# Full-array products and transposes as two column tiles of 64, and a new order of steps on all engines

## The chip, the cores and the metric

The kernel runs on one core of one Trainium2 chip. The metric is the time of one execution on the device, in microseconds (us), all input and output transfers between the chip's memory and the core included. Of several executions the median counts.

## The reference

Four layers follow one another on 16 images of 64 channels and 16 x 16 pixels, all in f32. The first is attention over channels, the second a deformable 3 x 3 convolution, the third attention over pixels, the fourth a block of normalisation, depthwise convolution, four gated one-dimensional convolutions and a gated feed-forward part.

```python
# L0: attention over channels
q, k, v = (einsum('oc,bcn->bon', w, x) + b for (w, b) in (q, k, v))
attn = softmax(einsum('bcn,bdn->bcd', q, k) / sqrt(64))
x = x + einsum('bcd,bdn->bcn', attn, v)
# L1: deformable 3x3 convolution, batch norm, relu
om = conv3x3(x, w_off) + b_off                  # 18 offsets and 9 masks per pixel
sampled = bilinear(x, grid + tap + om[:18]) * sigmoid(om[18:])
x = relu(batch_norm(einsum('bckhw,ock->bohw', sampled, w_dcn) + b_dcn))
# L2: attention over the 256 pixels
q, k, v = (einsum('oc,bcn->bon', w, x) + b for (w, b) in (q, k, v))
attn = softmax(einsum('bci,bcj->bij', q, k) / 8)
x = x + einsum('oc,bcn->bon', wp, einsum('bij,bcj->bci', attn, v)) + bp
# L3
y = depthwise3x3(ln2d(x)) + dw_b
o = sum over left-right, right-left, top-bottom, bottom-top of conv5(y) * sigmoid(G y + g)
x = x + fuse(o)
z = ff1(ln2d(x)); a, g = split(z)
x = x + ff2(a * sigmoid(g))
```

## The kernel before, in words

Two images make a pair: 2 x 64 channels fill the 128 partitions and 256 pixels lie in the free dimension, so 8 pairs (n = 1 to 8) go through the same steps. There is no loop over pairs. `PLAN` (lines 53 to 124) holds for each of the four engines one list of tokens such as `qk.4`, a step and its pair; `walk` (146) plays the list in that order, and the steps of several pairs are interwoven in it. Between engines every step waits on counting semaphores. SyncE (SP) loads the parameters, then for n = 3 to 8 loads pair n (333) and, from n = 6 on, first stores pair n - 5 (337).

TensorE's (PE's) steps and what they fill, with the lines of their products:

- `prep` (357, 358): once, the product of the weights v_w and p_w and of p_w with a bias. It needs the last parameter transfer, `par_late`.
- `qk` (366), `attn` (375), `at` (383), `mix` (390, 391), `x1` (397): layer 0. `at` transposes the normalised attention matrix, `mix` multiplies it with wv and leaves one 128 x 128 matrix that `x1` applies to both images.
- `off` (407), `off_t` (415): the offset convolution in nine taps and two halves, and its transpose. From it DVE (`dist`, `hat`, `hat_y`, and `low` once), ACT (`tanh`, `abs`, `high`) and POOL (`low`) make hat functions of the sampling positions, as an f16 high part and an f16 remainder in the tile `parts`.
- `tr0`, `tr1`, `tr2` (431): these parts transposed to `hats`, eight, eight and four f16 transposes of 128 x 128.
- `wx0`, `wx1`, `wx2` (446): x1 times the weights of the nine taps.
- `sp0` to `sp8` (`spread`, 460 and 455): selector products that spread the hats over all pixels, in f16 with 32 rows. ACT copies one of the two factors out (`xe`, 702), DVE multiplies them (`w0a` to `w8b`, 863), two products of 128 x 512 per tap.
- `s0a` to `s8b` (500): per tap and half two products, one for each image, that sum the samples in `cv`. `relu` (709) closes layer 1.
- `qk2` (511, 512), `v2` (521), `logit` (532), `et0` and `et1` (542, four f32 transposes each), `av` (553): layer 2.
- `gate` (564), `scan` (577), `fuse` (586), `ff` (597), `ff2` (605): layer 3. Its statistics and normalisation take DVE (`st1`, `st2`), POOL (`ln1`, `ln2`) and ACT (`ln1`, `ln2`), the depthwise taps ACT (`dw`) and DVE (`dw2` to `dw8`, `y`), and `x3`, `x4`, `prod`, `u` and `out` are DVE's.

A product uses part of the 128 x 128 array according to its operands: rows by the partitions it sums over, columns by the partitions it writes. In the profile "128*64" stands for 128 rows and 64 columns. This program uses four such shapes: 128*128 (prep, qk, x1, off_t, tr, qk2, v2, et), 128*64 (attn, at, off, s, av, fuse, ff2: two column tiles side by side, except at), 64*128 (mix, wx, logit, gate, scan, ff: two row tiles but for mix) and 32*128 (sp). An f32 product shows as two records, an f32 or f16 transpose as one. `nc.tensor.transpose` passes the data through in one pass, `nc.tensor.matmul` with an identity multiplies.

PSUM is small: nearly all steps of layers 0, 2 and 3 share the bank `mb` or the two banks `pair`. `turn` (151) lets a step write its bank only when the step before it in PE's list that used the same bank has been read by its last reader (`DONE`, 130):

```python
    turns = [entry for entry in entries(PLAN["pe"]) if entry[0] in BANK[bank]]
    at = turns.index((step, n))
    if at > 0:
        name, m = turns[at - 1]
        eng.wait_ge(semaphores[DONE[name]], m)
```

## Time and profile before

| | us |
|---|---|
| median of 3 runs | 326.28 |
| lowest, highest | 324.72, 327.69 |
| the profiled execution | 325.18 |
| its span, from the first to the last instruction | 323.3 |

All rows of the trace come from the one profiled execution and count from its span's start. The engines are PE (TensorE, matmul), PEld (its weight loads, which overlap PE), DVE (VectorE), ACT (ScalarE), POOL (GpSimd) and SP (SyncE). L500 is line 500 of the kernel. PE's records are drawn longer than the time for which one holds the engine back, because products are pipelined; the distance from the start of one step to the start of the next, or a piece of the chain of waits, is the better measure. The chain of waits is the work that ended last, followed back from the last instruction.

### The profile page before, as it was taken

How to read it: one execution, taken by the hardware profiler on the slowest of the kernel's cores; microseconds unless marked ns; L12 is line 12 of the kernel's file. 1: busy time of each engine (PE TensorE's matmuls, PEld its weight loads, DVE VectorE, ACT ScalarE, POOL GpSimd, SP SyncE). 2: the span in 40 equal slices, each digit the busy share in tenths (PEclk: the TensorE clock that was granted, in tenths of full speed). 3: DMA queues.
4: the chain of work that ended last, by engine and by line, in shares of the span. 5: the costliest groups of instructions: out<-in, count | busy, mean ns of one | idle time of the engine just before them, and what ended most of it. 6: DMA issues, size and time to landing. Idle time of an engine off the chain costs nothing.

```text
span 323.3 us, 6448 instructions
## 1 busy us (share of the span) xinstructions
PE 288.7 (89%) x2396; PEld 175.6 (54%) x2396; DVE 213.0 (66%) x422; ACT 192.4 (59%) x399; POOL 55.8 (17%) x139
## 2 busy tenths in 40 slices
...
GB/s 248 84 16 2 16 2 20 0 2 2 0 0 2 4 1 2 0 34 0 2 1 34 3 0 2 32 2 1 2 2 16 3 0 18 1 0 2 16 0 32
DMA packets 3053, 4.91 MB, mean 15 GB/s; under 512 B 336, under 2 KB 2768, under 8 KB 2896
## 3 DMA queue, kind: packets, MB, share of 16 engines
...
q14 instruction: 10, 0.08, 0.1%
...
## 4 chain that ended last, share of the span: by engine, by line
PE 74%; DVE 10%; ACT 6%; DMA 4%; issue 3%; POOL 1%; SPq 1%; DVEq 0%; POOLq 0%; ACTq 0%
PE ps_cv L500 20%; PE ps_pair L577 10%; PE ps_yb L460 7%; PE ps_pair L446 5%; PE ps_ma L407 4%; PE ps_mb L542 3%; PE ps_pair L532 3%; PE ps_ma L431 3%; PE ps_pair L564 3%; DMA sb_par<-in_par 2%; PE ps_pair L597 2%; PE ps_mb L553 2%; DVE sb_dw_acc L904 2%; DVE sb_wt L863 2%; PE ps_mb L586 2%
## 5 line engine op out<-in xcount | busy, mean ns | idle before, releaser
L863 DVE TENSOR_TENSOR sb_wt<-ps_yb,sb_xe 128x512 f32<-128x512 f32 x144 | 94.1, 686 | 34.1 <-PE ps_xb L455 32.8
L500 PE MATMUL ps_cv<-sb_wt,sb_w_x 128*64 128x256 f32 x576 | 81.2, 393 | 0.6 <-DVE sb_wt L863 0.5
L702 ACT ACTIVATE sb_xe<-ps_xb 128x512 f32<-128x512 f32 x72 | 42.9, 595 | 13.6 <-PE ps_xb L455 13.5
L500 PEld LDWEIGHTS ps_cv<-sb_wt,sb_w_x 128*64 128x64 f32 x576 | 34.4, 136 | 26.2 <-issue 12.6
L577 PE MATMUL ps_pair<-sb_y_pad,sb_par 64*128 64x256 f32 x320 | 37.6, 385 | 0.0
L999 POOL TENSOR_TENSOR sb_parts<-sb_hat,sb_parts 128x256 f16<-128x256 f32 (+2 forms) x40 | 24.3, 639 | 73.6 <-ACT sb_parts L672 73.6
L577 PEld LDWEIGHTS ps_pair<-sb_y_pad,sb_par 64*128 64x128 f32 x320 | 30.1, 186 | 7.1 <-issue 2.8
L904 DVE SCALAR_TENSOR_TENSOR sb_dw_acc<-sb_z_pad,sb_par,sb_dw_acc 128x256 f32<-128x256 f32 x56 | 26.1, 506 | 11.3 <-ACT sb_dw_acc L754 7.5
L460 PE MATMUL ps_yb<-sb_hats,sb_sel 32*128 32x512 f16 x144 | 29.8, 384 | 1.5 <-DVE sb_wt L863 1.1
L455 PE MATMUL ps_xb<-sb_hats,sb_sel 32*128 32x512 f16 x72 | 27.7, 385 | 0.1
L1006 POOL TENSOR_SCALAR sb_sc<-sb_mv 128x1 f32<-128x1 f32 x16 | 4.4, 277 | 133.5 <-DVE sb_mv L898 77.2
L446 PE MATMUL ps_pair<-sb_par,sb_x 64*128 64x256 f32 (+1 forms) x192 | 23.6, 362 | 0.7 <-ACT sb_w_x L692 0.6
L681 ACT ACTIVATE sb_hats<-ps_ma 128x1024 f16<-128x1024 f16 (+1 forms) x24 | 21.1, 880 | 4.7 <-PE ps_ma L431 4.6
L692 ACT ACTIVATE sb_w_x<-ps_pair 128x1024 f32<-128x1024 f32 (+1 forms) x24 | 19.4, 809 | 7.5 <-PE ps_pair L446 7.2
L460 PEld LDWEIGHTS ps_yb<-sb_hats,sb_sel 32*128 32x128 f16 x144 | 7.2, 91 | 23.4 <-issue 20.1
L446 PEld LDWEIGHTS ps_pair<-sb_par,sb_x 64*128 64x128 f32 x192 | 15.5, 186 | 7.2 <-issue 6.1
L407 PE MATMUL ps_ma<-sb_x_pad,sb_par 128*64 128x128 f32 x288 | 18.7, 287 | 0.6 <-DVE sb_x_pad L825 0.6
L407 PEld LDWEIGHTS ps_ma<-sb_x_pad,sb_par 128*64 128x64 f32 x288 | 16.8, 144 | 3.0 <-DVE sb_x_pad L825 1.8
L731 ACT ACTIVATE sb_b_exp<-ps_pair,sb_b_neg 128x256 f32<-128x256 f32 x32 | 14.7, 476 | 4.9 <-DVE sb_b_neg L872 4.9
L770 ACT ACTIVATE sb_conv<-ps_pair,sb_par 128x512 f32<-128x512 f32 x16 | 10.1, 682 | 9.2 <-PE ps_pair L577 9.2
L597 PE MATMUL ps_pair<-sb_z,sb_par 64*128 64x256 f32 x64 | 10.2, 439 | 5.9 <-ACT sb_z L777 4.0
L834 DVE TENSOR_TENSOR sb_dist<-ps_ma,sb_grid 128x1152 f32<-128x1152 f32 x8 | 10.8, 1352 | 5.7 <-PE ps_ma L415 5.6
...
## 6 DMA issues: line engine op xcount, KB each, us to landing
...
```

The costliest lines, as they stand in the source:

```text
L407: mm = nc.tensor.matmul(ma[C * h:C * (h + 1), 0:P], par_sb[:, a + 2 * OM * t:a + 2 * OM * (t + 1)], x1_pad[:, r:r + HALF_ROWS, t % 3:t % 3 ...
L446: mm = nc.tensor.matmul(pair[:, 512 * b + PIX * h:512 * b + PIX * h + k], x1[r, P * h:P * (h + 1)], par_sb[r, a:a + k], start=True, stop=True)
L455: return nc.tensor.matmul(xb[:, :], sel_sb[rows, P:2 * P], hats[n % 2][rows, g, :], start=True, stop=True)
L460: return nc.tensor.matmul(yb[h][:, :], sel_sb[rows, P * (2 + h):P * (3 + h)], hats[n % 2][rows, g, :], start=True, stop=True)
L500: mm = nc.tensor.matmul(cv[C * b:C * (b + 1), 0:PIX], w_x[n % 2][:, b, h, k, :], wt_of(n, k, h)[:, PIX * b:PIX * (b + 1)], start=(k == 0 a ...
L577: mm = nc.tensor.matmul(pair[:, 512 * b + PIX * d:512 * b + PIX * (d + 1)], par_sb[r, a:a + P], rows, start=(j == 0), stop=(j == KS - 1))
L681: nc.scalar.activation(hats[n % 2][:, g0:g1, :].rearrange("p g q -> p (g q)"), ma[:, :].bitcast(F16)[:, 0:k], ACT.Copy).then_inc(ev(f"hats ...
L692: nc.scalar.activation(w_x[n % 2][:, :, :, t0:t1, :].rearrange("p b h t c -> p b h (t c)"), pair[:, :].rearrange("p (b h q) -> p b h q", b ...
L702: nc.scalar.activation(xe[t % XE][:, :], xb[:, :], ACT.Copy).then_inc(ev("xe_ok"), 1)
L863: nc.vector.tensor_tensor(wt_of(n, k, h)[:, :], yb[h][:, :], xe[t % XE][:, :], ALU.mult)\
L904: nc.vector.scalar_tensor_tensor(out=sum_of, in0=dw_source(t), scalar=col("dw_w", t), in1=sum_of, op0=ALU.mult, op1=ALU.add).then_inc(ev(f ...
L999: nc.gpsimd.tensor_tensor(parts[:, 0:g, a:b, 1, :], hat[:, 0:g, a:b, :], parts[:, 0:g, a:b, 0, :], ALU.subtract).then_inc(ev("low_ok"), 1)
```

## The change

Seven kinds of PE steps that used the full array now issue each product twice, for columns 0 to 63 and 64 to 127 of the stationary operand, into partitions 0 to 63 and 64 to 127 of PSUM: prep, qk, x1, off_t, tr, qk2, v2. mix does the same and sums over 128 rows instead of 64; for that `at_sb` has 128 rows, whose lower half a sixth memset on DVE clears. at and off_t use a product with the identity instead of the transpose. et0 and et1 keep the full array. The f16 transposes of tr stay transposes, each as two of half width.

All four lists of `PLAN` hold the same tokens as before in a new order. Below are the lines of the lists that matter here, then the whole code part.

```diff
     "pe": """
-        qk.1 attn.1 prep.1 at.1 mix.1 x1.1 off.1 off_t.1 qk.2 attn.2 wx0.1 qk.3 wx1.1 at.2 tr0.1 wx2.1 mix.2 sp_first.1
 ...
-        scan.2 sp1.5 qk2.4 s0a.5 s0b.5 at.6 logit.4 mix.6 sp2.5 tr2.5 x1.6 s1a.5 off.6 sp3.5 fuse.2 off_t.6 s1b.5 wx1.6
-        v2.4 sp4.5 s2a.5 s2b.5 wx0.6 sp5.5 s3a.5 s3b.5 et0.4 s4a.5 wx2.6 sp6.5 et1.4 ff.2 s4b.5 s5a.5 s5b.5 sp7.5 gate.3
 ...
-        ff2.5 s7b.8 sp_last.8 av.7 s8a.8 s8b.8 scan.6 qk2.8 logit.8 fuse.6 v2.8 et0.8 gate.7 et1.8 ff.6 av.8 scan.7
-        ff2.6 gate.8 fuse.7 scan.8 ff.7 fuse.8 ff.8 ff2.7 ff2.8
+        qk.1 attn.1 at.1 mix.1 x1.1 prep.1 off.1 off_t.1 qk.2 attn.2 wx0.1 wx1.1 qk.3 tr0.1 at.2 mix.2 wx2.1 sp_first.1
 ...
+        attn.6 gate.2 qk2.4 tr2.5 s0b.5 sp2.5 s1a.5 at.6 mix.6 logit.4 fuse.2 s1b.5 sp3.5 x1.6 s2a.5 off.6 wx1.6 sp4.5
+        et0.4 off_t.6 wx2.6 v2.4 wx0.6 sp5.5 et1.4 s2b.5 ff.2 s3a.5 s3b.5 av.4 ff2.2 sp6.5 gate.3 s4a.5 s4b.5 s5a.5
 ...
+        s7a.8 av.7 s7b.8 sp_last.8 gate.6 s8a.8 ff2.5 s8b.8 scan.6 qk2.8 logit.8 fuse.6 v2.8 et0.8 gate.7 et1.8 av.8
+        ff.6 scan.7 ff2.6 gate.8 fuse.7 scan.8 fuse.8 ff.7 ff.8 ff2.7 ff2.8
     """,
     "act": """
-        attn.1 prep.1 at.1 mix.1 off.1 tanh.1 abs.1 attn.2 wx0.1 high.1 wx1.1 at.2 tr0.1 wx2.1 mix.2 xe0.1 tr1.1 xe1.1
 ...
-        exp0.8 v2.8 exp1.8 ln2.6 et0.8 gate.7 et1.8 ff.6 ln1.8 dw.8 scan.7 gate.8 ln2.7 scan.8 ff.7 ln2.8 ff.8
+        attn.1 at.1 mix.1 prep.1 off.1 abs.1 tanh.1 attn.2 wx0.1 high.1 wx1.1 at.2 tr0.1 mix.2 xe0.1 tr1.1 xe1.1 wx2.1
 ...
+        k2.8 exp0.8 v2.8 exp1.8 et0.8 et1.8 gate.7 ln2.6 ff.6 ln1.8 dw.8 scan.7 gate.8 ln2.7 scan.8 ff.7 ln2.8 ff.8
     """,
     "dve": """
-        qk.1 a_max.1 a_norm.1 x1.1 dist.1 qk.2 a_max.2 hat.1 hat_y.1 qk.3 a_norm.2 low.1 w0a.1 x1.2 w0b.1
 ...
-        w4b.5 w5a.5 y.3 hat.6 hat_y.6 w5b.5 w6a.5 u.2 w6b.5 out.2 w7a.5 x3.4 st1.4 qk.7 w7b.5 w8a.5 dw2.4 dw4.4 dw3.4
-        out.6 x4.7 st2.7 prod.8 x4.8 st2.8 u.7 out.7 u.8 out.8
+        qk.1 a_max.1 a_norm.1 x1.1 dist.1 qk.2 a_max.2 hat.1 hat_y.1 a_norm.2 low.1 qk.3 x1.2 a_max.3 w0a.1 w0b.1
 ...
+        w3b.5 w4a.5 dw2.3 dist.6 dw4.3 dw6.3 w4b.5 w5a.5 dw8.3 dw3.3 dw5.3 hat.6 dw7.3 u.2 x3.4 y.3 st1.4 out.2 hat_y.6
+        dw4.8 dw5.8 dw6.8 dw7.8 dw8.8 out.6 y.8 prod.7 x4.7 st2.7 prod.8 x4.8 st2.8 u.7 out.7 u.8 out.8
     """,
     "pool": """
-        grid.1 x1.1 bn.1 low.1 x1.2 low.2 x1.3 low.3 x1.4 ln1.1 low.4 ln1.2 x1.5 low.5 ln2.1
-        ln1.3 x1.6 ln2.2 low.6 ln1.4 ln2.3 x1.7 low.7 x1.8 ln1.5 ln2.4 low.8 ln1.6 ln2.5 ln1.7
-        ln2.6 ln1.8 ln2.7 ln2.8
+        x1.1 grid.1 bn.1 low.1 x1.2 low.2 x1.3 x1.4 low.3 low.4 ln1.1 ln1.2 x1.5 ln2.1 low.5 ln1.3 x1.6 ln2.2 ln1.4
+        low.6 ln2.3 x1.7 low.7 x1.8 ln1.5 ln2.4 low.8 ln1.6 ln2.5 ln1.7 ln2.6 ln1.8 ln2.7 ln2.8
     """,
 ...
@@ -188,7 +186,7 @@
         a_sum = sb("a_sum", [P, 1])
         a_rec = sb("a_rec", [P, 1])
         a_nrm = sb("a_nrm", [P, C])
-        at_sb = sb("at", [C, P])
+        at_sb = sb("at", [P, P])
         mix = sb("mix", [P, P])
         mix_b = sb("mix_b", [P, 1])
         x1 = sb("x1", [P, PIX])
@@ -350,21 +348,30 @@
             ident = part("ident")
             ident16 = sel_sb[:, 0:P]
 
+            def columns_of(t):
+                return slice(C * t, C * (t + 1))
+
             def prep(n):
                 if n == 1:
                     pe.wait_ge(par_late, 16)
                     turn(pe, S, "mb", "prep", n)
-                    nc.tensor.matmul(mb[:, 0:P], part("v_w"), part("p_w"), start=True, stop=True)
-                    nc.tensor.matmul(mb[:, P:P + 1], part("p_w"), col("v_b"), start=True, stop=True)\
-                        .then_inc(prep_mm, 1)
+                    for t in range(2):
+                        nc.tensor.matmul(mb[columns_of(t), 0:P], part("v_w")[:, columns_of(t)], part("p_w"),
+                                         start=True, stop=True)
+                    for t in range(2):
+                        mm = nc.tensor.matmul(mb[columns_of(t), P:P + 1], part("p_w")[:, columns_of(t)], col("v_b"),
+                                              start=True, stop=True)
+                    mm.then_inc(prep_mm, 1)
 
             def qk(n):
                 once(pe, n, 1, par_first, 16)
                 pe.wait_ge(x_loaded[n % 2], 16 * ((n + 1) // 2))
                 turn(pe, S, "mb", "qk", n)
                 for h in range(HALVES):
-                    mm = nc.tensor.matmul(mb[:, 2 * P * h:2 * P * (h + 1)], x_in[n % 2][:, P * h:P * (h + 1)],
-                                          part("qk_w"), start=True, stop=True)
+                    for t in range(2):
+                        mm = nc.tensor.matmul(mb[columns_of(t), 2 * P * h:2 * P * (h + 1)],
+                                              x_in[n % 2][:, P * h + C * t:P * h + C * (t + 1)],
+                                              part("qk_w"), start=True, stop=True)
                 mm.then_inc(ev("qk_mm"), 1)
 
             def attn(n):
@@ -380,22 +387,29 @@
                 once(pe, n, 1, par_first, 32)
                 pe.wait_ge(ev("a_nrm_ok"), n)
                 turn(pe, S, "mb", "at", n)
-                nc.tensor.transpose(mb[0:C, 0:P], a_nrm[:, :], ident).then_inc(ev("at_mm"), 1)
+                nc.tensor.matmul(mb[0:C, 0:P], a_nrm[:, :], ident, start=True, stop=True).then_inc(ev("at_mm"), 1)
 
             def mix_step(n):
                 once(pe, n, 1, par_in, 16)
+                once(pe, n, 1, zero_ok, 6)
                 pe.wait_ge(ev("at_ok"), n)
                 turn(pe, S, "mb", "mix", n)
                 a, b = AT["av_w"]
-                nc.tensor.matmul(mb[:, 0:P], par_sb[0:C, a:b - 1], at_sb[:, :], start=True, stop=True)
-                nc.tensor.matmul(mb[:, P:P + 1], at_sb[:, :], par_sb[0:C, b - 1:b], start=True, stop=True)\
-                    .then_inc(ev("mix_mm"), 1)
+                for t in range(2):
+                    nc.tensor.matmul(mb[columns_of(t), 0:P], par_sb[:, a + C * t:a + C * (t + 1)], at_sb[:, :],
+                                     start=True, stop=True)
+                for t in range(2):
+                    mm = nc.tensor.matmul(mb[columns_of(t), P:P + 1], at_sb[:, columns_of(t)], par_sb[:, b - 1:b],
+                                          start=True, stop=True)
+                mm.then_inc(ev("mix_mm"), 1)
 
             def x1_step(n):
                 pe.wait_ge(ev("mix_ok"), n)
                 turn(pe, S, "mb", "x1", n)
-                nc.tensor.matmul(mb[:, 0:PIX], mix[:, :], x_in[n % 2][:, :], start=True, stop=True)\
-                    .then_inc(ev("x1_mm"), 1)
+                for t in range(2):
+                    mm = nc.tensor.matmul(mb[columns_of(t), 0:PIX], mix[:, columns_of(t)], x_in[n % 2][:, :],
+                                          start=True, stop=True)
+                mm.then_inc(ev("x1_mm"), 1)
 
             def off_step(n):
                 pe.wait_ge(ev("x1_pad_ok"), n)
@@ -412,7 +426,9 @@
 
             def off_t(n):
                 pe.wait_ge(ev("off_ok"), n)
-                nc.tensor.transpose(ma[:, 0:P], off[:, :], ident).then_inc(ev("pos_mm"), 1)
+                for t in range(2):
+                    mm = nc.tensor.matmul(ma[columns_of(t), 0:P], off[:, columns_of(t)], ident, start=True, stop=True)
+                mm.then_inc(ev("pos_mm"), 1)
 
             def tr(g0, g1, index):
                 def step(n):
@@ -428,8 +444,10 @@
                         for b in range(2):
                             for h in range(HALVES):
                                 at = 2 * PIX * (g - g0) + PIX * b + P * h
-                                mm = nc.tensor.transpose(bk[:, at:at + P], parts[:, 2 * h + b, 4 * g:4 * g + 4, :, :],
-                                                         ident16)
+                                for t in range(2):
+                                    mm = nc.tensor.transpose(bk[columns_of(t), at:at + P],
+                                                             parts[:, 2 * h + b, 4 * g + 2 * t:4 * g + 2 * (t + 1), :, :],
+                                                             ident16)
                     mm.then_inc(ev(f"tr_mm{index}"), 1)
                 return step
 
@@ -508,9 +526,11 @@
                 once(pe, n, 1, prep_act, 5)
                 once(pe, n, 1, ev("prep_ok"), 1)
                 turn(pe, S, "mb", "qk2", n)
-                nc.tensor.matmul(mb[:, 0:PIX], part("q_w"), x2[n % 3][:, :], start=True, stop=True)
-                nc.tensor.matmul(mb[:, PIX:2 * PIX], part("k_w"), x2[n % 3][:, :], start=True, stop=True)\
-                    .then_inc(ev("qk2_mm"), 1)
+                for j, w in enumerate((part("q_w"), part("k_w"))):
+                    for t in range(2):
+                        mm = nc.tensor.matmul(mb[columns_of(t), PIX * j:PIX * (j + 1)], w[:, columns_of(t)],
+                                              x2[n % 3][:, :], start=True, stop=True)
+                mm.then_inc(ev("qk2_mm"), 1)
 
             def v2_step(n):
                 pe.wait_ge(ev("x2_ok"), n)
@@ -518,8 +538,10 @@
                 once(pe, n, 1, ev("prep_ok"), 1)
                 turn(pe, S, "mb", "v2", n)
                 for h in range(HALVES):
-                    mm = nc.tensor.matmul(mb[:, P * h:P * (h + 1)], x2[n % 3][:, P * h:P * (h + 1)], pv_w[:, :],
-                                          start=True, stop=True)
+                    for t in range(2):
+                        mm = nc.tensor.matmul(mb[columns_of(t), P * h:P * (h + 1)],
+                                              x2[n % 3][:, P * h + C * t:P * h + C * (t + 1)], pv_w[:, :],
+                                              start=True, stop=True)
                 mm.then_inc(ev("v2_mm"), 1)
 
             def logit(n):
@@ -640,10 +662,10 @@
 
             def attn_t(n):
                 act.wait_ge(ev("at_mm"), n)
-                nc.scalar.activation(at_sb[:, :], mb[0:C, 0:P], ACT.Copy).then_inc(ev("at_ok"), 1)
+                nc.scalar.activation(at_sb[0:C, :], mb[0:C, 0:P], ACT.Copy).then_inc(ev("at_ok"), 1)
 
             def mix_step(n):
-                once(act, n, 1, zero_ok, 5)
+                once(act, n, 1, zero_ok, 6)
                 act.wait_ge(ev("mix_mm"), n)
                 for b in range(2):
                     r = slice(C * b, C * (b + 1))
@@ -959,7 +981,8 @@
             nc.vector.memset(y_pad[:, :, :], 0.0).then_inc(zero_ok, 1)
             nc.vector.memset(parts[:, :, AXES:4 * GROUPS, :, :], 0.0).then_inc(zero_ok, 1)
             nc.vector.memset(x1_pad[:, :, :], 0.0).then_inc(zero_ok, 1)
-            dve.wait_ge(zero_ok, 5)
+            nc.vector.memset(at_sb[C:P, :], 0.0).then_inc(zero_ok, 1)
+            dve.wait_ge(zero_ok, 6)
             walk(PLAN["dve"], steps)
 
         @block.gpsimd
```

## Rows read from the trace of the kernel before

**Rows 1.** Profile page, part 1: busy us, share of the span, instructions.
```profile
PE 288.7 (89%) x2396; PEld 175.6 (54%) x2396; DVE 213.0 (66%) x422; ACT 192.4 (59%) x399; POOL 55.8 (17%) x139
```
**Rows 2.** Stretches: length, busy time per engine, granted PE clock, DMA share.
```profile
40.00:280.00 240.00, 235.80 (x2011) 141.28 (x2011) 179.97 (x350) 161.27 (x330) 42.45 (x101) 1.00 0.02 6
...
285.80:292.70 6.90, 6.49 (x30) 3.46 (x30) 0.39 (x2) 4.10 (x7) 0.17 (x1) 0.53 0.00 0
```
**Rows 3.** Waits of the whole span: total us, times, longest.
```profile
DVE sb_wt L863 <- PE ps_xb L455: 32.8, 35, 4.7
```
**Rows 4.** Chain of waits (start us, us, what), pieces of column and 32-row tiles.
```profile
60.84 0.58 PE ps_cv L500 x4
...
85.91 0.32 PE ps_yb L460 x2
...
86.24 1.01 PE ps_mb L553 x8
87.25 0.86 PE ps_cv L500 x8
```
**Rows 5.** Chain of waits, pieces of full-array and row-tiled steps.
```profile
59.78 1.06 PE ps_mb L366 x4
...
61.42 1.06 PE ps_pair L446 x8
62.48 0.63 PE ps_mb L397 x2
...
82.51 0.59 PE ps_mb L542 x4
...
195.84 0.49 PE ps_mb L397 x2
```
**Rows 6.** Chain of waits, the f16 transposes of tr.
```profile
72.69 0.55 PE ps_ma L431 x8
...
74.81 0.45 PE ps_ma L431 x8
...
76.74 0.33 PE ps_ma L431 x4
```
**Rows 7.** Timeline of PE (start us, us): small column tiles, then off.2.
```profile
33.93 0.45 PE L375 MATMUL ps_mb<-sb_qk 128*64 128x64 f32 x8
...
34.18 2.17 PE L407 MATMUL ps_ma<-sb_x_pad,sb_par 128*64 128x128 f32 x36
```
**Rows 8.** Groups of weight loads: busy us, mean ns, idle before.
```profile
L431 PEld LDWEIGHTS ps_ma<-sb_sel,sb_parts 128*128 128x128 f16 x160 | 9.3, 98 | 8.0 <-issue 6.5 <-ACT sb_hats L681 1.4
...
L375 PEld LDWEIGHTS ps_mb<-sb_qk 128*64 128x64 f32 x64 | 2.9, 146 | 4.9 <-DVE sb_qk L802 3.9 <-issue 0.9
```
**Rows 9.** Timeline of the start, all engines.
```profile
6.03 2.14 POOL L984 TENSOR_TENSOR sb_grid<-sb_par 128x1152 f32<-128x1152 f32 x1 [5.22 <-DMA sb_par<-in_par]
...
8.20 0.26 DVE L818 TENSOR_SCALAR sb_a_nrm<-sb_a_exp,sb_a_rec 128x64 f32<-128x64 f32 x1
...
11.24 0.79 PE L357 MATMUL ps_mb<-sb_par 128*128 128x128 f32 x2 [4.17 <-DMA sb_par<-in_par]
...
11.82 0.43 PE L358 MATMUL ps_mb<-sb_par 128*128 128x1 f32 x2
...
12.86 0.39 PE L383 MATMUL ps_mb<-sb_par,sb_a_nrm 128*64 128x128 f32 x1 [0.61 <-ACT sb_pv_b L633]
...
17.33 3.42 PE L407 MATMUL ps_ma<-sb_x_pad,sb_par 128*64 128x128 f32 x36 [0.58 <-DVE sb_x_pad L825]
```
**Rows 10.** Chain of waits in the tail: ff.6 and av.8.
```profile
288.77 2.08 PE ps_pair L597 x8
290.85 1.93 PE ps_mb L553 x8
```
**Rows 11.** Timeline: out.2 on DVE and qk.7 on PE.
```profile
203.36 0.47 DVE L946 SCALAR_TENSOR_TENSOR sb_y_out<-ps_mb,sb_par,sb_x 128x256 f32<-128x256 f32 x1
...
206.81 1.13 PE L366 MATMUL ps_mb<-sb_par,sb_x_in 128*128 128x256 f32 x4 [0.36 <-DMA sb_x_in<-in_x]
```

More of the change, by code:

```diff
@@ L75 @@
[L75 to L77 removed]
+        qk.1 attn.1 at.1 mix.1 x1.1 prep.1 off.1 off_t.1 qk.2 attn.2 wx0.1 wx1.1 qk.3 tr0.1 at.2 mix.2 wx2.1 sp_first.1
+        x1.2 tr1.1 sp0.1 attn.3 tr2.1 sp1.1 wx2.2 off.2 sp2.1 at.3 s0a.1 s0b.1 off_t.2 mix.3 sp3.1 s1a.1 wx0.2 s1b.1
```

96 lines of the change are left out of this document (47 added, 49 removed).

## The prediction, made before the change was run

> **What bounds the kernel now.** The page comes first: TensorE (PE) is busy for 89% of the span, VectorE (DVE) for 66%, ScalarE (ACT) for 59% [rows 1]. An average over a start, a long middle and a tail says little, so the stretches come next: from 40 to 280 us PE is busy for 235.8 of 240 us, while DVE has 60 us free and ACT 79 [rows 2]. The waits agree: DVE's largest is for PE's spread products, 32.8 us [rows 3]. So in the middle whatever PE saves or adds counts in full; at both ends (0 to 40, 280 to 323) a chain through all engines sets the time.
>
> The chain of waits prices PE's steps, because where PE is full a piece lasts as long as its step holds PE back. A step of L500 (a pair of column tiles, four records of 256 columns) is 0.58 us. Eight such records (L553 has the same shape) take 1.01, so each further pair costs 0.43 and entering costs 0.15. The entry price vanishes where the step before has the same array shape: L500's eight records right behind L553 take 0.86. A spread step (512 f16 columns in 32-row tiles) is 0.32 [rows 4]. Full-array steps pay more on entry: L366 is 1.06 for two streams of 0.43 (0.21 on entry), L397 0.63 (0.20), the four transposes of L542 0.59 (0.16). L397 behind another full-array step is 0.49: 0.14 of its entry goes there too. The row-tiled L446 is 1.06, 0.21 above its stream [rows 5].
>
> **The order of PE's steps, counted.** I take the stretch of the PE list from wx0.2 to scan.6, which lay between 41 and 273 us. In the old list 267 of its 357 steps follow one of another shape: 93 enter 128x64, 47 64x128, 68 the 32-row shape and 59 128x128 (13 et, 20 tr, 6 off_t, 20 of qk, x1, qk2, v2). In the new list 205 of 357 do: 79, 43, 69 and 14 (only et0 and et1 stay full). The old order with the new shapes gives 212, the new order with the old shapes 248: most of it comes from the shapes.
>
> The prices: 0.153 into 128x64 (also et and off_t), 0.21 into 64x128 and for full products, 0.10 for tr (below), and 0.32 less 512 f16 columns at 0.42 ns = 0.105 for the spread. Old: 93 x 0.153 + 47 x 0.21 + 68 x 0.105 + 19 x 0.153 + 20 x 0.10 + 20 x 0.21 = 40.3 us. New: 79 x 0.153 + 43 x 0.21 + 69 x 0.105 + 14 x 0.153 = 30.5. Saved: 9.8 us.
>
> **What the conversion adds.** qk, x1, qk2 and v2 stream as many columns as before, two tiles at a time as L500 and L553 do: nothing. off_t and at leave the one-pass transpose (a quarter of L542's 0.43, 0.107) for a product with the identity in two passes: 0.213, 11 such steps, +1.2 us. mix gets two one-column records more, +0.1 in all. The f16 transposes are the open item. The old tr of eight is 0.55 after another shape and 0.45 after the same, the one of four 0.33 [rows 6]: 0.056 per transpose (128 columns at 0.44 ns) plus 0.10. Now there are 16 of half width. No f16 column tile is in the trace. The nearest is L375, in f32 column tiles of 64 with a stream of 64 columns (64 f32 columns at 0.43/512 us last 54 ns, as 128 f16 columns do): its eight records held PE for 34.18 - 33.93 = 0.25 us before a step of the same shape, 31 ns each [rows 7]. So a tr of eight is 16 x 0.031 = 0.50 us, against 0.45 without entry: +0.05 fourteen times, +0.025 seven times, +0.9 us. Bounds: at pure stream, 8 x 0.054 = 0.43, it would be -0.4 us in the stretch; if each half transpose needed a whole one's 56 ns, 0.90, it would be +7.9. I take 0.50: the same tile, the same stream.
>
> A rule of the Trainium skill speaks against this step: "TensorEngine Tiling (Array Packing)", Restrictions and Gotchas, says that column tiling excludes fast weight load, and "TensorE: Matmul & The Clock Gate", on the weight-path modes, that fast load serves 128 weights that aren't fp32. The rows allow it: a load of 128 f16 columns lasts 98 ns, one of 64 f32 columns 146 [rows 8], so by the rule half the columns may load in more time. By it the tr of eight is anything up to the upper bound above.
>
> Middle: -9.8 + 1.2 + 0.1 + 0.9 = **-7.6 us**.
>
> **The start.** a_nrm.1 is ready at 8.46, but PE stands in prep.1, which waits for the last parameter transfer until 11.24; at.1 starts at 12.86, off.1 at 17.33. With prep.1 behind x1.1, at.1 can start at 8.6, 4.26 earlier; the transfer that mix needs was in by 6.03, when POOL began grid.1 [rows 9]. Prep's own products (11.24 to 12.25) then stand ahead of off.1, and at and off_t have a pass more, slow here (L407 takes 3.42 us, and 2.17 later [rows 7]). So: -4.26 + 1.0 + 0.35 = **-2.9 us**. POOL now runs x1.1 before grid.1: hidden, x1.1 ends near 13.6, grid.1 lasts 2.1, and dist.1 needs it near 18.5; uncovered, it would cost those 2.1. The sixth memset lies before 3 us, under the first load. qk.3 behind wx1.1 and tanh behind abs lie beside the hat and low chain on ACT, DVE and POOL: nothing.
>
> **The tail.** The old chain goes through ff.6 (288.77, 2.08 us) and then av.8 (1.93), which heads the last image's long path [rows 10]. The new list has av.8 before ff.6, and ACT copies et1.8 before it does the gates. ff.6 then lies beside the norm and the seven dw steps. That removes 2.08 us as profiled, about 1.07 at the middle's speed: PE's granted clock averages 0.53 from 285.8 to 292.7, mostly 1.2 GHz instead of 2.4, after PE had idled before it [rows 2]. ACT's gates leave the path too (up to -0.7 net of et1's copy). Against that, out.6 now stands before y.8 on DVE and waits for ff2.6 behind scan.7: up to +0.5. Together **-2.0 us**. ff.7 behind fuse.8 is hidden by the statistics of x4.8.
>
> **What is late next.** SP loads image n behind the store of image n-5, so qk.6, qk.7 and qk.8 wait for out.1, out.2 and out.3, two DMA issues and a landing. out.2 begins at 203.36 and qk.7 at 206.81, 3.45 us, and PE had idled 0.36 for it [rows 11]. In the new list PE has s7b, sp and scan (5.3 us) between ff2.1 and qk.6; sp, gate, four s and sp (3.6) between ff2.2 and qk.7; two wx, two s and v2 (3.6) between ff2.3 and qk.8. out.2 has x3.4, y.3 and st1.4 ahead of it, about three times its own 0.47, of which 0.4 lie beside ff2.2: it begins 1.1 after ff2.2 and qk.7 is free 4.5 after it, 0.9 late instead of 0.36. qk.6 and qk.8 come out even. **+0.5 us.**
>
> **Sum.** -7.6 - 2.9 - 2.0 + 0.5 = -12.0 us. The profiled execution took 325.18 us (its span 323.3 and 1.9 around it): 313.2. The median of the runs shown is 326.28, 1.1 above it, so the forecast is 314.2 us. Its own range is 309.5 to 318.5: downward the lower bound of tr (-0.5), a tail at full clock (-3) and a start without the slow passes (-1); upward 4 us of new waits, as much as PE idles in the middle now.
>
> **Rivals.** (a) Half transposes aren't faster than whole ones: +0.40 x 16 + 0.20 x 8 = 8.0 us over all images, **322.2 us**. For it: 320 instructions where 160 were, and slower loads. Against: L375's 31 ns. "TensorE: Matmul & The Clock Gate", Part 1, names about 62 ns of sequencer time per MATMUL under one decode setting; if two f32 records are one instruction, L375's 0.25 us is that very limit, and the skill's figure would make 320 transposes 19.8 us long, this rival again. Chance 0.14.
> (b) The new order leaves PE waiting: PE has less to do per tap, and DVE's two products with ACT's copy hold the spread chain. For it: DVE is 75% busy in the middle. If each of the 72 taps waits for 0.07 us more, that is 5: **319.2 us**. Chance 0.10.
> (c) Slower than before: two column tiles that stream the *same* operand (x_in, x2, the identity) run one after the other. Place: qk, x1, qk2, v2. Price: 0.86 + 0.43 + 0.86 + 0.43 = 2.58 us per pair of images, 20.6 in all: **334.8 us**. It decides once 60% of the overlap there is lost. For it: the pairs of rows 4 stream different operands. Against: L500's pairs share one bank and a step as these do, and overlap fully. Chance 0.04.
> The forecast keeps 0.72.
>
> **Chances.** A change of 1%, 3.3 us, is about what a measurement of this kernel can tell from none. The forecast is faster but for 0.01; (a) lies on the bound (0.09 faster, 0.05 same); (b) gives 0.08 and 0.02; (c) is slower: faster 0.88, same 0.08, slower 0.04. The range, 309.5 to 322.2, reaches to (a).
>
> **What would show it.** PE has 2736 matmul records instead of 2396. In the chain, qk2 and qk take 0.86 behind an L500 step and 1.01 behind others, x1 0.43 or 0.58, a tr of eight 0.50 or 0.65. at.1 begins near 8.6, off.1 near 14.4, the span is about 311, and PE's share of the middle stays at 98%. Wrong if a tr of eight takes 0.9 (a), if PE's share of the middle falls below 96% (b), if qk takes 1.9 (c), if off.1 starts at 17, or if PE waits more than 1 us for an x_in.

## The result, and the profile after

The changed kernel takes 322.48 us (median of four runs, 322.19 to 323.02); the kernel before, run beside it, 326.67. The ratio is 0.988, with a 95% interval of 0.983 to 0.993. So it is faster by 1.2%, where 3.7% was forecast, and it ends 0.3 us outside the range. The profiled execution took 322.19 us with a span of 320.4, 2.9 less than the 323.3 of before. A median here and below is over all executions, while a ratio leaves out those that ran in the chip's slower state, so the two need not agree.

The page after, part 1 and a row of part 2 (40 slices of 8 us), against [rows 1]:

```profile
PE 282.3 (88%) x2736; PEld 179.4 (56%) x2736; DVE 211.4 (66%) x423; ACT 191.7 (60%) x399; POOL 52.8 (16%) x139
...
PEclk9999999999999999999999999999999999999955
```

PE's work shrank by 6.4 us, its records grew to 2736 as forecast, and yet the span shrank by only 2.9. PE's share fell. Where it fell, the stretches say (busy us and records per engine, granted clock, DMA share), against [rows 2]:

```profile
40.00:280.00 240.00, 228.90 (x2284) 143.26 (x2280) 179.40 (x352) 159.50 (x330) 40.46 (x101) 1.00 0.02 7
```

In the middle PE is busy for 228.9 us where it was 235.8: it idles 11.1 us instead of 4.2. That is 95.4%, under the 96% that the prediction had named as the sign of rival (b). Who it waits for there, in the view of waits over 40 to 280 us (total us, times, longest), with DVE's and ACT's largest waits below:

```profile
PE ps_yb L478 <- DVE sb_wt L885: 3.9, 12, 0.5
...
DVE sb_wt L885 <- PE ps_xb L473: 31.8, 33, 4.0
...
ACT sb_xe L724 <- PE ps_xb L473: 20.5, 24, 2.0
```

L478 is a spread step's row products, L885 DVE's product of a tap. In the same stretch of before PE waited for that product 0.9 us in two waits, DVE for PE 27.4 us and ACT 13.5. Now each engine of the tap loop waits more for the others: no engine has become the bound.

The prices of PE's steps are as the prediction had them, or lower. Pieces of the chain (start us, us, what), against [rows 4 to 6]:

```profile
30.10 0.45 PE ps_ma L448 x16
...
85.32 1.01 PE ps_mb L531 x8
86.34 0.86 PE ps_cv L518 x8
...
90.79 0.57 PE ps_ma L448 x16
...
96.93 0.43 PE ps_mb L410 x4
```

qk2 (L531) takes 1.01 behind another shape; L518 takes 0.86 behind it, without entry price; x1 (L410) takes 0.43. A tr of sixteen half transposes (L448) takes 0.45 among steps of its shape and 0.57 to 0.64 at a change, where eight whole ones take 0.45 and 0.55 in [rows 6]. So rival (a), 0.9, falls; 1.01 instead of 1.9 for a step of eight records is the end of rival (c).

The two ends. First pieces of the timeline at the start, against [rows 7, 9]:

```profile
8.53 0.66 PE L390 MATMUL ps_mb<-sb_par,sb_a_nrm 128*64 128x128 f32 x2 [1.48 <-DVE sb_a_nrm L840]
...
13.85 4.12 PE L421 MATMUL ps_ma<-sb_x_pad,sb_par 128*64 128x128 f32 x36
...
33.39 2.19 PE L421 MATMUL ps_ma<-sb_x_pad,sb_par 128*64 128x128 f32 x36
```

at.1 starts at 8.53 and off.1 at 13.85, 3.5 earlier than before. But off.1 takes 4.12 us instead of 3.42, and off.2, at 33.39, is only 0.8 earlier than in [rows 7]. The longer off.1 isn't a cost of the change: its instructions are those of before, and experiment 5, whose PE list and shapes are the changed kernel's up to there, shows it at 3.37 us:

```profile
13.88 3.37 PE L423 MATMUL ps_ma<-sb_x_pad,sb_par 128*64 128x128 f32 x36
```

Then the chain of the last 15 us:

```profile
306.47 1.97 PE ps_mb L608 x8
308.45 2.03 PE ps_pair L619 x8
310.48 0.02 issue
310.50 0.69 ACT sb_ff_a L806
311.19 0.58 ACT sb_ff_g L807
311.77 0.50 ACT sb_z L799
312.26 0.04 issue
312.31 2.08 PE ps_pair L619 x8
```

fuse.8 (L608) and both last ff steps (L619) take twice what they take in the middle, at a granted clock of 0.5, the lower of the two levels, 1.2 GHz. The clock is there from 306 us to the end. ff.7 stands on the chain between fuse.8 and ff.8.

Where three steps start tells how the 2.9 us came about (us, from the timelines). The first is only a rough mark between kernels whose order differs: in the new order wx2.2 and at.3 stand ahead of it and off_t.2 behind it, which by the pieces of the chain is some 0.5 us more work done.

| | before | after | new shapes, old order | the same with the new ends |
|---|---|---|---|---|
| s0a.1, first sample step | 37.1 | 35.8 | 38.9 | 37.0 |
| scan.6 | 273.4 | 271.4 | 270.5 | 267.3 |
| end of the span | 323.3 | 320.4 | 320.0 | 315.0 |
| so: start, middle, tail | | -1.2, -0.8, -0.9 | +1.8, -4.7, -0.4 | -0.1, -6.0, -2.2 |

The last two columns are the first and third experiment. The start of the last one is not a fair sample: from 28 to 36 us the granted clock of its profiled execution averages 0.57. off.2 takes 3.38 us in it, and 2.19 in experiment 6, which up to there differs only in `at`:

```profile
32.88 3.38 PE L423 MATMUL ps_ma<-sb_x_pad,sb_par 128*64 128x128 f32 x36
```

```profile
31.48 2.19 PE L423 MATMUL ps_ma<-sb_x_pad,sb_par 128*64 128x128 f32 x36
```

Without that stretch s0a.1 begins at 34.4 (experiment 6) and 34.7 (experiment 9, the same lists), and scan.6 at 265.8 and 264.9.

### The profile page after: what moved, and what is told of

The parts are those of the page before. It is cut to its first block, busy times and chain, and to the rows that moved or that the text cites. A ratio compares the mean times of both kernels' runs of the same rounds, so it can differ in the third digit from the quotient of the medians.

```text
span 320.4 us, 7130 instructions
## 1 busy us (share of the span) xinstructions
PE 282.3 (88%) x2736; PEld 179.4 (56%) x2736; DVE 211.4 (66%) x423; ACT 191.7 (60%) x399; POOL 52.8 (16%) x139
## 4 chain that ended last, share of the span: by engine, by line
PE 63%; DVE 17%; issue 10%; ACT 7%; POOL 1%; DMA 1%; DVEq 0%; SPq 0%; POOLq 0%; ACTq 0%
PE ps_cv L518 14%; PE ps_pair L599 12%; PE ps_yb L478 6%; DVE sb_wt L885 5%; PE ps_ma L421 5%; PE ps_pair L464 4%; PE ps_pair L619 3%; PE ps_ma L448 3%; DVE sb_dw_acc L926 3%; PE ps_mb L564 2%; PE ps_mb L372 2%; PE ps_pair L586 2%; PE ps_pair L554 2%; DVE sb_prod L941 1%; PE ps_mb L410 1%
## 5 line engine op out<-in xcount | busy, mean ns | idle before, releaser
L885 DVE TENSOR_TENSOR sb_wt<-ps_yb,sb_xe 128x512 f32<-128x512 f32 x144 | 94.3, 685 | 35.4 <-PE ps_xb L473 33.7
L518 PE MATMUL ps_cv<-sb_wt,sb_w_x 128*64 128x256 f32 x576 | 77.3, 386 | 0.0
L518 PEld LDWEIGHTS ps_cv<-sb_wt,sb_w_x 128*64 128x64 f32 x576 | 37.2, 136 | 21.5 <-issue 8.7
L599 PEld LDWEIGHTS ps_pair<-sb_y_pad,sb_par 64*128 64x128 f32 x320 | 32.2, 184 | 7.3 <-issue 4.4
L478 PE MATMUL ps_yb<-sb_hats,sb_sel 32*128 32x512 f16 x144 | 29.8, 381 | 5.3 <-DVE sb_wt L885 4.3
L1022 POOL TENSOR_TENSOR sb_parts<-sb_hat,sb_parts 128x256 f16<-128x256 f32 (+2 forms) x40 | 23.1, 610 | 51.8 <-ACT sb_parts L694 51.8
L478 PEld LDWEIGHTS ps_yb<-sb_hats,sb_sel 32*128 32x128 f16 x144 | 7.7, 91 | 28.8 <-issue 24.1
L792 ACT ACTIVATE sb_conv<-ps_pair,sb_par 128x512 f32<-128x512 f32 x16 | 10.1, 684 | 17.1 <-PE ps_pair L599 17.1
L421 PE MATMUL ps_ma<-sb_x_pad,sb_par 128*64 128x128 f32 x288 | 19.4, 293 | 0.2
L421 PEld LDWEIGHTS ps_ma<-sb_x_pad,sb_par 128*64 128x64 f32 x288 | 17.5, 147 | 2.0 <-DVE sb_x_pad L847 1.1
L448 PE MATMUL ps_ma<-sb_sel,sb_parts 128*64 128x128 f16 x320 | 13.7, 221 | 1.7 <-POOL sb_parts L1022 1.3
```

What stands on the lines that cost most here:

```text
L421: mm = nc.tensor.matmul(ma[C * h:C * (h + 1), 0:P], par_sb[:, a + 2 * OM * t:a + 2 * OM * (t + 1)], x1_pad[:, r:r + HALF_ROWS, t % 3:t % 3 ...
L448: mm = nc.tensor.transpose(bk[columns_of(t), at:at + P], parts[:, 2 * h + b, 4 * g + 2 * t:4 * g + 2 * (t + 1), :, :], ident16)
L478: return nc.tensor.matmul(yb[h][:, :], sel_sb[rows, P * (2 + h):P * (3 + h)], hats[n % 2][rows, g, :], start=True, stop=True)
L518: mm = nc.tensor.matmul(cv[C * b:C * (b + 1), 0:PIX], w_x[n % 2][:, b, h, k, :], wt_of(n, k, h)[:, PIX * b:PIX * (b + 1)], start=(k == 0 a ...
L599: mm = nc.tensor.matmul(pair[:, 512 * b + PIX * d:512 * b + PIX * (d + 1)], par_sb[r, a:a + P], rows, start=(j == 0), stop=(j == KS - 1))
L885: nc.vector.tensor_tensor(wt_of(n, k, h)[:, :], yb[h][:, :], xe[t % XE][:, :], ALU.mult)\
```

## The experiments

In what follows the first number is the median of the executions, and the ratio is to the kernel before, run beside it. "The middle" is the time from the start of s0a.1 to that of scan.6, 236.3 us before and 235.5 in the changed kernel.

**1. The new shapes in the old order.**

```diff
-PLAN = the new lists
+PLAN = the lists of the kernel before, all four engines
```

> All of the changed kernel's products in column tiles, but the four lists of steps as before. Theory O (the new order gives back what the shapes save): the shape entries avoided are worth 7 to 9 us in the middle, the old order lets PE stay full, and its start and tail are unchanged: 317.5 to 320 us, ratio to before 0.973 to 0.98, scan.6 begins 7 to 9 us before 273.4. Theory L (a quicker PE cannot be used in any order, since the loop PE, ACT, DVE, PE then sets the pace): 322 to 325 us, and PE's share from 80 to 280 falls to about 95% as in the changed kernel.

Measured: 319.88 us, 0.974 (0.968 to 0.981). With the old order the kernel is faster than with the order that was laid out for it. The time is where Theory O put it, but scan.6 begins only 2.9 us earlier than before, not 7 to 9, and from 80 to 280 us PE is busy for 193.3 us where it was 196.4. So a part of what the shapes save is idle time in the old order too. PE waits for a tap's product at the spread's rows for 1.4 us in three waits between 40 and 280 us.

**2. The new order with the old shapes.**

```diff
-PLAN = the lists of the kernel before
+PLAN = the new lists, in the kernel before
```

> The changed kernel's four lists with the full-array products and transposes of before. Theory O: 267 entries become 248, worth 2.8 us, start and tail win 3 to 5 us, and the order's own waits (about 8 us more than before) eat it: 324 to 329 us, and PE idles in the middle as in the changed kernel (share near 96%). Theory L: with PE slow again the waits go, PE's share is back at 98%, and start and tail show: 319 to 322 us.

Measured: 329.2 us (324.9 to 333.7 in eleven executions), 1.000 (0.995 to 1.005). The order alone brings nothing, though it has fewer changes of shape and the earlier start. In the profiled execution, a long one of 332.2 us with its start at the lower clock, the middle ran at a granted clock of 1.00 and can be compared: it takes 239.9 us, 3.6 more than before. With the new shapes the new order costs 235.5 - 231.6 = 3.9. So its price doesn't come from the quicker PE.

**3. The old order with the new start and end.**

```diff
 pe:   qk.1 attn.1 -prep.1- at.1 mix.1 x1.1 +prep.1+ off.1   ...  gate.7 et1.8 +av.8+ ff.6 -av.8-
 act:  attn.1 -prep.1- at.1 mix.1 +prep.1+ off.1             ...  -ln2.6- et0.8 +et1.8+ gate.7 +ln2.6+ -et1.8- ff.6
 pool: +x1.1+ grid.1 -x1.1-
```

> As the first, but with the lists' edits at both ends: prep.1 behind x1.1 on PE and ACT, x1.1 before grid.1 on POOL, av.8 before ff.6 on PE, et1.8 before gate.7 and ln2.6 after it on ACT. Theory O: 3 us more than the first at the start and 1 to 2 in the tail: 313 to 316 us. Theory L: the start's gain is used up in the middle: within 1.5 us of the first.

Measured: 315.64 us, 0.965 (0.959 to 0.970), a span of 315.0. The new ends take another 1.0% off experiment 1 (the two intervals just overlap), and the middle stays as good as there. The stretch and the wait, as above:

```profile
40.00:280.00 240.00, 232.50 (x2322) 143.50 (x2324) 185.18 (x364) 163.76 (x340) 44.37 (x106) 1.00 0.02 7
```

```profile
PE ps_yb L480 <- DVE sb_wt L887: 1.2, 2, 0.6
...
DVE sb_wt L887 <- PE ps_xb L475: 23.7, 30, 4.7
...
ACT sb_xe L726 <- PE ps_xb L475: 11.4, 16, 3.0
```

PE gets through 2322 records of the same 2736 in the stretch in which the changed kernel gets through 2284, and all three waits of the tap loop are shorter. These are the same instructions in the same shapes: the order is the difference. Over the whole kernel it costs 5.4 us by the two spans, 6.8 by the medians and 7.6 by the ratios (2.4%, give or take 0.7). scan.6 begins 4.1 us later in the changed kernel than here, and 5.5 and 6.5 later than in experiments 6 and 9; in the middle itself the difference is 4.1 to 5.3. It isn't one place. PE's busy time in 40 us each, first of this kernel, then of the changed one:

```profile
40.00:80.00 40.00, 39.43 (x457) 1.00 0.02 5
80.00:120.00 40.00, 38.56 (x380) 1.00 0.01 2
120.00:160.00 40.00, 38.95 (x387) 1.00 0.03 8
160.00:200.00 40.00, 39.72 (x389) 1.00 0.03 8
200.00:240.00 40.00, 39.04 (x415) 1.00 0.04 11
```

```profile
40.00:80.00 40.00, 39.02 (x447) 1.00 0.02 5
80.00:120.00 40.00, 37.81 (x375) 1.00 0.01 2
120.00:160.00 40.00, 37.93 (x375) 1.00 0.03 8
160.00:200.00 40.00, 38.53 (x384) 1.00 0.03 8
200.00:240.00 40.00, 38.21 (x401) 1.00 0.03 8
```

Each 40 us lose 0.4 to 1.2. Experiments 4, 7, 10, 11 and 12 move steps within one list to ask how, and 8 and 9 add buffers; 5 and 6 price two of the conversions.

**4. Sixteen spreads one step later,** in PE's list of the changed kernel. These are the spreads before which PE had waited.

```diff
-... wx1.2 sp5.1 tr0.2 ... x1.4 sp3.2 s0a.2 ...
+... wx1.2 tr0.2 sp5.1 ... x1.4 s0a.2 sp3.2 ...
```

> The changed kernel with 16 spread steps of PE's list, those before which PE had waited 0.14 to 0.53 us, each moved behind the one step that follows it; nothing else. In the changed kernel these waits sum to 5.3 us of the 18.4 us by which PE's steps from 40 to 280 us held it longer than their prices. Theory S (the spread steps stand too early in PE's list, and PE could do the next step meanwhile): 3 to 5 us less, 317.5 to 320 us. Theory D (DVE and ACT come late with their own work, wherever PE's spread stands): the wait moves to the next spread, and the entries into the 32-row shape rise: within 1 us of the changed kernel's 322.5, or above it.

Measured: 326.38 us, 0.998 (0.994 to 1.002). The wait at the spreads' rows does shrink, from 3.9 to 2.6 us, and the time still rises by 1%. The middle takes 240.1 us, 4.5 more than the changed kernel's; of that, PE being busy 2.5 us longer goes with a stretch at a lower clock in this execution (0.52 and 0.63 from 88 to 92 us), and 2.0 are idle time. What the spreads feed is now late. PE in 40 to 280 us:

```profile
PE ps_yb L481 <- DVE sb_wt L888: 2.6, 5, 0.9
PE ps_pair L467 <- ACT sb_w_x L717: 2.0, 2, 1.7
PE ps_ma L451 <- POOL sb_parts L1025: 1.8, 2, 1.1
```

**5. The old order with the new ends, tr in the full array.**

```diff
-for t in range(2):
-    mm = nc.tensor.transpose(bk[columns_of(t), at:at + P], parts[:, 2 * h + b, 4 * g + 2 * t:4 * g + 2 * (t + 1), :, :], ident16)
+mm = nc.tensor.transpose(bk[:, at:at + P], parts[:, 2 * h + b, 4 * g:4 * g + 4, :, :], ident16)
```

> The kernel e3_shapes_old_order_ends with the f16 transposes of tr in the full array again (8, 8, 4 of them per pair of images instead of 16, 16, 8 of half width). If the half transposes are as cheap as the trace shows (16 in 0.45 us between steps of the same shape, 0.45 for eight whole ones plus entries), the full ones cost their own entry of 0.10 and the 0.15 of the column step behind them: 24 x 0.10 plus about 12 x 0.15 = 4 us more, 318 to 320 us against 315.6. If their number of instructions mattered, it would be level or faster.

Measured: 320.31 us, 0.977 (0.971 to 0.983), against 0.965 for experiment 3. So the half transposes, twice as many instructions, are worth 1.3%, some 4 us. The middle says the same: 235.2 us here, 230.3 and 231.4 in experiments 3 and 6, so 3.8 to 4.9. That is most of the 4.7 to 6.1 us that all new shapes save there in the old order.

**6. The same kernel as 3, at as a one-pass transpose.**

```diff
-nc.tensor.matmul(mb[0:C, 0:P], a_nrm[:, :], ident, start=True, stop=True)
+nc.tensor.transpose(mb[0:C, 0:P], a_nrm[:, :], ident)
```

> The kernel e3_shapes_old_order_ends with at as the one-pass transpose of before (it fills 64 columns either way). Each at holds PE 0.11 us shorter: 0.9 us in all if PE is the bound, 314.7 us against 315.6; that is below what the runs resolve in the time, so the piece of at in the trace decides: 0.11 against 0.21 us between steps of one shape.

Measured: 317.45 us, 0.965 (0.959 to 0.971): no difference in the time. In the timeline an at holds PE for 53.15 - 52.92 = 0.23 us before the sample step behind it:

```profile
52.92 0.30 PE L392 MATMUL ps_mb<-sb_par,sb_a_nrm 128*64 128x128 f32 x1
53.15 1.52 PE L520 MATMUL ps_cv<-sb_wt,sb_w_x 128*64 128x256 f32 x12
```

In experiment 3 the same place shows 55.77 - 55.50 = 0.27. The second pass costs 0.04 there, not the 0.1 that the prediction gave it. Before a step of another shape, the logit at 146.9, an at holds PE for 0.34 in experiment 3 and 0.20 here: there it costs 0.14.

**7. The sixteen spreads one step earlier.**

```diff
-... wx1.2 sp5.1 tr0.2 ... x1.4 sp3.2 s0a.2 ...
+... sp5.1 wx1.2 tr0.2 ... sp3.2 x1.4 s0a.2 ...
```

> The changed kernel, with the same sixteen spreads that stood late in the last run (sp5.1 sp3.2 sp2.3 sp3.3 sp7.3 sp2.4 sp4.4 sp5.4 sp1.6 sp8.6 sp4.7 sp6.7 sp7.7 sp0.8 sp5.8 sp6.8) each moved one step ahead in TensorE's list instead of one step behind. Theory D (the loop from a spread over ACT's copy and the vector engine's two products to the next spread sets the pace of the middle, and the new order gives it too little lead): 318 to 320.5 us, TensorE busy in 80:280 goes from 189.9 to 191 to 193 us, and its waits for the vector engine's products at the spreads' rows line from 3.9 us to under 2.5. Theory S2 (the loop is not what is short of time; TensorE waits wherever the vector engine does a burst of other work): 321.5 to 324, the same waits at steps one further. Theory E (these steps are already as early as their operands allow, so that one step earlier adds waits): over 324.

Measured: 335.31 us (four executions from 331.4 to 380.4, of which the ratio rests on two), 1.015 (1.010 to 1.021); in the profile, one of those two, a span of 329.7, 9.3 more than the changed kernel's, and a middle of 246.2, 10.6 more. PE in 40 to 280 us:

```profile
PE ps_yb L478 <- DVE sb_wt L885: 14.0, 16, 1.5
```

14.0 us in sixteen waits, as many as spreads were moved: +10.1 against 3.9, which is about the added time. That is Theory E. Theory D falls: moving these sixteen in PE's list alone gives no lead.

**8 and 9. More buffers,** in the changed kernel and in that of experiment 3.

```diff
-RING = 6
-XE = 3
+RING = 8
+XE = 4
```

> The changed kernel with four buffers instead of three for ACT's copy of the column spread and eight instead of six for the products. Nothing else differs. If the new order's lost time comes from the ring being full (ACT's copy waiting for a free buffer, a product waiting for the sample matmuls): 318 to 320.5 us, and ACT's idle before the copy falls. If it is the latency round the loop of one tap, in which the buffers take no part: 321.5 to 323.5, with TensorE busy 189.9 of 200 us in 80:280 as before.

> The new shapes in the old order with the new ends (315.6 us when it ran), with four and eight buffers instead of three and six. Its TensorE is busy 193.1 us of 200 in 80:280, so there is little for a buffer to give: 314.5 to 316.5 us. Under 314 would say that the ring takes part in what is left of TensorE's waits even in the old order.

Measured: 321.04 us, 0.981 (0.977 to 0.986), and 315.9 us, 0.967 (0.962 to 0.972). The intervals overlap those without the buffers (0.988 and 0.965). In 8, PE's wait at the spreads' rows is 3.8 us in twelve waits, ACT's before its copy 20.3 and the middle 235.1 us, as in the changed kernel; in 9 the middle is 230.2, as in experiment 3. Buffers aren't what is short in the middle; the times alone, between the two that were expected, leave room for a gain of up to 1.4% in the changed kernel.

**10 and 11. Evenly spaced spreads,** in the changed kernel and in that of experiment 3.

```diff
 26 spreads each, by one to three steps; in 10 for instance
-... s8a.6 x1.8 sp0.7 off.8 et0.5 off_t.8 s8b.6 sp1.7 et1.5 ...
+... s8a.6 x1.8 off.8 sp0.7 et0.5 off_t.8 s8b.6 et1.5 sp1.7 ...
```

> The changed kernel with 26 of the 73 spreads moved by one to three steps in TensorE's list, some ahead and some behind, so that the work between one spread and the next is nowhere short where it can be helped. By the durations of the chain, the changed order has 15 stretches between two spreads with under 1.5 us of other work for TensorE (the old order has 4), and this one has 3. Theory G (a spread can't follow the one before it sooner than ACT's copy and two products of the vector engine allow, about 1.8 us after it, so short stretches cost and long ones give nothing back): waits at the spreads' rows line for the products 40:280 go from 3.9 us to under 1.5, time 317.5 to 320.5 us. Theory B (the vector engine's bursts of other work in the new order hold the products, wherever the spreads stand): the waits stay at 3 us or more, 321.5 to 324 us.

> The new shapes in the old order with the new ends (315.6 us when it ran), with 26 spreads moved in the same way. The old order has only 4 stretches under 1.5 us, two of them at the start where nothing can be done, so Theory G gives it at most 1 us: 314.5 to 316.5 us. Under 314 us would say that the unevenness costs beyond the waits; over 317 that moving spreads costs something of its own.

Measured: 328.18 us, 1.003 (1.000 to 1.007), and 326.22 us, 0.997 (0.993 to 1.000). Both are far off what was expected: 1.5% and 3.3% slower than their own starting points (middles of 240.2 and 240.1 us). Theory G falls. In experiment 11, PE in 40 to 280 us:

```profile
PE ps_yb L480 <- DVE sb_wt L887: 2.7, 3, 1.1
PE ps_mb L566 <- DVE sb_b_nrm L906: 2.5, 2, 1.5
PE ps_cv L520 <- DVE sb_wt L887: 2.3, 5, 1.0
PE ps_mb L374 <- DMA sb_x_in<-in_x: 2.2, 2, 1.9
```

A sample step, an et step and a qk step wait now, each in its own place. The old order too is spoilt by moving spreads alone; uneven spacing isn't what either order suffers from.

**12. DVE's products ahead of other work.**

```diff
 dve, at sixteen places, for instance
-... w0a.3 nrm1.1 hat.4 w0b.3 w1a.3 w1b.3 w2a.3 x3.1 ...   -... w8b.5 y.4 w0a.6 prod.3 ...
+... w0a.3 nrm1.1 w0b.3 w1a.3 w1b.3 w2a.3 hat.4 x3.1 ...   +... w8b.5 w0a.6 y.4 prod.3 ...
```

> The changed kernel with the vector engine's list alone altered: at the sixteen spreads of the fourth run, the one piece of other work that stands right ahead of the products that the spread waits for (x1.3, qk.5, hat.4 twice, max.2, dist.5, hat.5, dw6.2, y.4, qk.8, hat_y.8, st2.4 twice, nrm0.6, prod.5, max.7) is put behind them. TensorE's list is as in the changed kernel. Theory B (in the new order the vector engine comes to these products too late, because other work stands ahead of them): TensorE's waits at the spreads' rows line 40:280 fall from 3.9 us to under 1.5, and the time to 318 to 320.5 us. Theory J (the four lists fit each other step by step, and any one of them moved alone costs, as with the spreads): 323 to 332 us, with new waits at the steps that were put behind.

Measured: 329.58 us, 1.006 (1.002 to 1.011), 1.8% slower than the changed kernel: Theory J. PE in 40 to 280 us:

```profile
PE ps_yb L480 <- DVE sb_wt L887: 3.0, 7, 0.7
PE ps_ma L450 <- POOL sb_parts L1024: 2.8, 3, 1.9
PE ps_mb L566 <- DVE sb_b_nrm L906: 1.5, 1, 1.5
PE ps_cv L520 <- DVE sb_wt L887: 1.4, 1, 1.4
```

The wait at the spreads shrinks by 0.9 us only, and tr (L450) and et (L566) now wait for the hats and norms that were put behind.

**All middles side by side** (us, from s0a.1 to scan.6 of each profiled execution; the granted clock is 1.00 in all but 4):

| | middle | PE busy | PE idle |
|---|---|---|---|
| before | 236.3 | 232.8 | 3.5 |
| 2: old shapes, new order | 239.9 | 231.1 | 8.8 |
| the changed kernel | 235.5 | 225.5 | 10.0 |
| 8: more buffers in it | 235.1 | 225.4 | 9.7 |
| 1: new shapes, old order | 231.6 | 225.6 | 6.0 |
| 3; 6; 9: new ends too | 230.3; 231.4; 230.2 | 225.6; 225.5; 225.5 | 4.7; 6.0; 4.8 |
| 5: tr in the full array | 235.2 | 228.5 | 6.7 |
| 4: sixteen spreads later (lower clock from 88 to 92) | 240.1 | 228.0 | 12.1 |
| 7: sixteen spreads earlier | 246.2 | 226.0 | 20.2 |
| 10; 11: spreads evened | 240.2; 240.1 | 225.3; 225.9 | 15.0; 14.2 |
| 12: products ahead | 241.7 | 226.3 | 15.5 |

With the new shapes and the full clock PE is busy for 225.3 to 226.3 us in every order (tr in the full array apart), so what one order costs against another is PE's idle time.

## Why the prediction was wrong

**The step that failed is the one that the term "Middle" rests on: that "in the middle whatever PE saves or adds counts in full", with the new order costing nothing but its entries.** The prediction took 7.6 us off the middle. PE's own work did shrink by 7.3 (232.8 to 225.5 us busy), but the middle itself by 0.8 only, for PE's idle time in it went from 3.5 to 10.0 us. Two things are in that. The new order costs 3.9 us in the middle against the old one with the same shapes (experiment 1), 4.1 to 5.3 against experiments 3, 6 and 9, and 3.6 with the old shapes (experiment 2). And in the old order too, 1.2 to 2.5 of the 7 us that PE saves become idle time.

The forecast held 4 us of new waits to be the edge of its own range, and gave rival (b), 5 us of them, one chance in ten. In size (b) was about right, and its sign came true: PE busy for 95.4% of 40 to 280 us instead of 98. Its reason did not. It blamed the loop, with PE having less to do per tap. But in the old order PE has just as little to do per tap and waits 1.2 us instead of 3.9 for the products, and with the old shapes, where PE has more to do, the new order costs as much. It is the order. That experiment 3, with the order of before, comes out at 315.64 us, 1.4 above the forecast of 314.2, isn't a success of the sum: its span is 8.3 us shorter than before, not 12.0, for its start fell short by a stretch at the lower clock and its middle by 1.6 us. (The prediction's own addition is off by a little: 313.2 and 1.1 make 314.3, and the items of its range 309.7 and 318.2 instead of 309.5 and 318.5. Nothing hangs on it.)

Of the 9.1 us between the forecast of -12.0 and the -2.9 of the two spans, the middle makes 6.8, the start 1.7 and the tail 1.1; against them stand the 0.5 that the forecast had added for what is late next.

Point by point, by the prediction's own steps:
- **The entries (-9.8), and what the conversion adds (+2.2): right as a sum of PE's work,** -7.6 forecast and -7.3 measured. tr was mis-sized: a tr of sixteen takes 0.45 where 0.50 was taken, and 0.57 to 0.64 at a change where 0.65 was. The rule of the Trainium skill ("TensorEngine Tiling (Array Packing)", Restrictions and Gotchas) that column tiling excludes fast weight load had no price here. The rows do fit it, for a load of 64 f16 columns lasts 109 ns in the groups of after and one of 128 columns 98 in [rows 8], but between steps of one shape tr is no longer. Nor did the 62 ns per MATMUL show that the Trainium skill gives for one decode setting ("TensorE: Matmul & The Clock Gate", Part 1): sixteen in 0.45 us are 28 ns each.
- **The start (-2.9): right up to off.1, and nearly right with the old order.** at.1 started at 8.53 (forecast 8.6) and off.1 at 13.85, 0.5 earlier than forecast. By s0a.1 the changed kernel has 1.2 us left, or some 1.7 with the work that it has done beyond the mark. With the old order and the new ends it is 2.4 (experiment 9) and 2.7 (experiment 6); only experiment 3's own execution, with its stretch at the lower clock, shows 0.1. The +1.8 of experiment 1 isn't all shapes either: 0.7 of it arise in off.1, 4.11 us against 3.42 with the same instructions.
- **The tail (-2.0): the number met in experiment 3 (-2.2), missed in the changed kernel (-0.9), and in both the clock has a hand.** "ff.7 behind fuse.8 is hidden by the statistics" failed in the changed kernel, where ff.7's 2.03 us lie on the chain at the lower clock. It held in experiments 4 and 7, which end with the same steps: there fuse.8 takes 1.11 at the full clock, and the chain goes on through x4.8 and the statistics. Of experiment 7:

```profile
317.01 1.11 PE ps_mb L608 x8
318.12 0.03 issue
318.14 0.49 DVE sb_x L948
```

From scan.6 to the end experiments 4 and 7 take 47.9 and 47.8 us, as experiment 3 does with ff.7 ahead (47.7), against 49.0 in the changed kernel and 49.9 before. Where the clock fell twice in that part, experiments 6 and 10 take 49.8 with the new ends, no less than the 49.9 of before, where it also fell twice. So the swap by itself costs nothing, the 1.1 us or so go with the clock that fell early, and how much of the tail's gain is the lists' and how much the clock's stays open.
- **What is late next (+0.5): didn't happen.** PE has no wait for an x_in between 40 and 280 us in the changed kernel.
- **Rivals (a) and (c) fell** by the rows above, and by experiment 5, which gives the half transposes a gain.

What the new order gets wrong isn't one item. Five changes were made to single lists, spreads later, earlier, evened in both orders, and products ahead, and two to the buffers. Two explanations with a mechanism fell (spreads too early, by 4; too short a distance between them, by 10 and 11), and so did two more (too little lead, by 7; full buffers, by 8 and 9). Every reordering of one list cost 1.0 to 3.3%, in the old order too. The reading that fits all of this is that each list is fitted step by step to the other three, and that the old set fits better than the new one all along the middle; it is concluded from these failures, not shown by a run of its own. Which of the many meeting points between the new lists fall worst stays open; lists taken from both orders, engine by engine, were not run.
